# The passage from the bias stage to attention: earlier bias loads, the last third layer moved, another drain order

## What is computed

```
bias = jax.nn.relu(bias @ cpb_w1 + cpb_b1)
bias = jax.nn.relu(bias @ cpb_w2 + cpb_b2)
bias = (bias @ cpb_w3 + cpb_b3).reshape(b, GROUPS, H * W, Hd * Wd)
sim = jnp.einsum('bhid,bhjd->bhij', qh, kh) + bias
attn = jax.nn.softmax(sim, axis=-1)
out = jnp.einsum('bhij,bhjd->bhid', attn, vh)
```

## Time and profile before

| | us |
|---|---|
| time, median of 3 runs (2813.24 to 2814.31) | 2814.09 |
| the profiled execution's own time | 2813.33 |
| its span, first to last instruction | 2811.5 |
| TensorE busy in the span | 2704.1 (96%) |
| VectorE busy | 2146.4 (76%) |
| ScalarE busy | 1669.3 (59%) |
| GpSimd busy | 97.3 (3%) |

### The profile page before, as it was taken

How to read it: one execution, slowest core, us unless ns; L and a number is a source line. 1 busy time by engine, 2 the same in 40 slices (tenths; PEclk the granted TensorE clock), 3 DMA queues, 4 the chain that set the end, 5 groups by cost and what they waited for, 6 DMA issues and landing times. The chain is left out here.

```text
span 2811.5 us, 45931 instructions
## 1 busy us (share of the span) xinstructions
PE 2704.1 (96%) x20105; PEld 1351.6 (48%) x20105; DVE 2146.4 (76%) x1373; ACT 1669.3 (59%) x2594; POOL 97.3 (3%) x132
## 2 busy tenths in 40 slices
PE   5699999999999999999999999999799999999898
PEld 3434434444434444334444344444478888757553
DVE  5799999999999999999999999998552221224364
ACT  4677677776777777777777777776432222201244
POOL 3000000000000000000000000000421000000000
PEclk8899999999999999999999999999999999999999
DMA  1100000000000000001000000100600000200001
GB/s 71 56 16 30 8 29 30 16 29 9 29 29 16 30 9 29 29 16 30 9 29 29 16 29 11 33 7 1 198 1 1 0 1 1 86 0 1 1 1 60
DMA packets 38760, 72.26 MB, mean 26 GB/s; under 512 B 21088, under 2 KB 22048, under 8 KB 36896
## 3 DMA queue, kind: packets, MB, share of 16 engines
q1 hardware_dynamic: 38496, 69.19, 7.5%
q0 software_dynamic: 64, 0.13, 0.0%
HBM read 60.45 MB, written 8.86 MB: 25 GB/s over the span
## 5 line engine op out<-in xcount | busy, mean ns | idle before, releaser
L812 PE MATMUL l_ps<-mlp_w,W2H 128*64 128x512 f16 x5472 | 912.8, 392 | 1.7 <-DVE mlp_w L844 1.7
L889 ACT ACTIVATE relu_top<-l_ps 128x512 f32<-128x512 f32 x1024 | 612.1, 598 | 416.4 <-PE l_ps L812 371.6
L889 ACT ACTIVATE relu_bottom<-l_ps 128x512 f32<-128x512 f32 x1024 | 612.3, 598 | 78.8 <-PE l_ps L812 0.7
L830 DVE SCALAR_TENSOR_TENSOR relu_top<-relu_bottom,sign_ratio,relu_top 128x2048 f32<-128x2048 f32 x256 | 601.4, 2349 | 11.6 <-ACT relu_bottom L889 11.6
L812 PE MATMUL l_ps<-mlp_w,W2L 128*64 128x512 f16 x2736 | 536.0, 388 | 0.0
L812 PEld LDWEIGHTS l_ps<-mlp_w,W2H 128*64 128x64 f16 x5472 | 304.1, 108 | 357.4 <-issue 77.8
L812 PE MATMUL l_ps<-h_words,W2H 128*64 128x512 f16 x2720 | 453.1, 392 | 0.0
L844 DVE TENSOR_TENSOR mlp_w<-words_x,XN 128x2048 f32<-128x2048 f32 x172 | 391.6, 2287 | 24.6 <-PE l_ps L812 24.6
L844 DVE TENSOR_TENSOR mlp_w<-XN 128x2048 f32<-128x2048 f32 x170 | 387.0, 2289 | 19.4 <-PE l_ps L812 19.1
L812 PE MATMUL l_ps<-h_words,W2L 128*64 128x512 f16 x1360 | 266.1, 388 | 0.0
L788 PE MATMUL l_ps<-relu_top,W 128*32 128x512 f32 x2048 | 246.8, 599 | 2.8 <-DVE relu_top L830 2.8
(11 more groups left out here) (389 smaller groups left out, 2696.7 us busy)
## 6 DMA issues: line engine op xcount, KB each, us to landing
XN<-pos_table SPq DMA_DIRECT2D x64, 512.0 KB, 3.7
mlp_w<-in_mlp_w SPq DMA_DIRECT2D x8, 1024.0 KB, 12.6
X<-in_x SPq DMA_DIRECT2D x8, 512.0 KB, 7.6
bias_scratch<-XN SPq DMA_DIRECT2D x64, 64.0 KB, 2.1
mlp_w_hi<-bias_scratch SPq DMA_DIRECT2D x16, 256.0 KB, 3.9
out<-Q SPq DMA_DIRECT2D x16, 256.0 KB, 2.2
XN<-y_pieces SPq DMA_DIRECT2D x96, 12.0 KB
y_rows<-y_pieces SPq DMA_DIRECT2D x96, 12.0 KB
```

The source lines that it names most:

```text
L812: last = nc.tensor.matmul(out[q][a * DH:(a + 1) * DH, :], w[:, half], h[a][:, :, k], start=False, stop=stop, tile_position=(0, a * DH))
L830: nc.vector.scalar_tensor_tensor(tops[i % 3], bots[i % 2][:], K.RHO[:], tops[i % 3], ALU.mult, ALU.add).then_inc(folded, 1)
L889: nc.scalar.activation((bots[i % 2] if d else tops[i % 3])[:, r, BANK * u:BANK * (u + 1)], banks[BANK_OF[c % PER]][:], ACT.Relu).then_inc( ...
```

## The change

- `stage_bias` no longer ends with layers three of doubles 254 and 255, fold 255, the copy and store of pair 15, nor with a wait for all stores. They are functions now (`last_rows_...`), called in `stage_attention`: the fold first on VectorE; the third layers on TensorE behind s 0 and s 1; the copy first on ScalarE; the store first on SP.
- At its end SP of `stage_bias` waits for the stores of 14 pairs (in a total over 15), for the first layers of pairs 0 to 14 and for the coordinate words of all, and loads the bias of four units into four slots, carved from tables that the last pair no longer uses.
- Attention has four bias slots in place of two. The units run in another order (`UNITS`): image 0's four first, then image 1's.
- SP there: store of pair 15 (4 DMAs), output weights, then for units 4 to 7 two bias loads (after the add four units back) and one 1 MB part of MLP weights each; parts 1 and 3; part 0 after six adds, part 2 after eight.
- The drain: TensorE tr g+1 ahead of w g, ScalarE `at` g+1 ahead of merged g; w 5 and w 7 go into score bank 0, whose last scores are added by then. The high part of the first projection tile is made after `at` 6, with merged 3 as its condition. VectorE waits for GpSimd's last multiply before it makes the low part of the output weights.
- Semaphores of an earlier stage are merged (five into two), with the same waits.

The core of the diff. The bodies of `layer_three`, `fold`, `copy_rows` and `store` move out of the engines' functions unchanged, and the removed code of TensorE and ScalarE in attention is in the listing above.

```diff
+UNITS = [c * B + b for b in range(B) for c in range(CC)]
...
+    def last_rows_folded(dve):
+        fold(dve, DBL - 1)
+    def last_rows_summed(pe):
+        layer_three(pe, DBL - 2)
+        layer_three(pe, DBL - 1)
+    def last_rows_copied(act):
+        copy_rows(act, BG - 1)
+    def last_rows_stored(sp):
+        store(sp, BG - 1)
+        return stored, 16 * CH * BG
+    K.last_rows_folded, K.last_rows_summed = last_rows_folded, last_rows_summed
+    K.last_rows_copied, K.last_rows_stored = last_rows_copied, last_rows_stored
+    room = carver(T.x, T.val, T.co[0])
+    K.bias_in = [K.sem(f"bias_in{i}") for i in range(4)]
+    K.bias_slots = [room([P, HALF, PC, J]) for _ in range(4)]
...
-                store(bg)
+                if bg + 1 < BG:
+                    store(sp, bg)
                 if bg + 2 < BG:
                     coords(bg + 2, 0)
                     y_rows(bg + 2)
-            sp.wait_ge(stored, 16 * CH * BG)
+            sp.wait_ge(stored, 16 * CH * (BG - 2))
+            sp.wait_ge(h1, H * (BG - 1))
+            sp.wait_ge(words, JOBS * BG)
+            for g, slot in enumerate(K.bias_slots):
+                for h in range(HALF):
+                    sp.dma_start(slot[:, h], K.db[HALF * UNITS[g] + h].rearrange("(s p) j -> p s j", p=P)).then_inc(K.bias_in[g], 16)
...
@@ the end of the tensor block of stage_bias
-                    layer_three(i - 2)
-                    layer_three(i - 1)
-            layer_three(DBL - 2)
-            layer_three(DBL - 1)
+                    layer_three(pe, i - 2)
+                    layer_three(pe, i - 1)
...
-            for i in range(DBL - 3, DBL):
-                fold(i)
+            for i in range(DBL - 3, DBL - 1):
+                fold(dve, i)
...
-            copy_rows(BG - 1)
@@ stage_attention
-    bi = [room([P, HALF, PC, J]) for _ in range(2)]
+    bi = K.bias_slots
     sc = [room([P, PC, HALF, J]) for _ in range(4)]
+    pr = [room([P, PC, HALF, J]) for _ in range(2)]
     at = [room([P, HW]) for _ in range(2)]
-    pr = [room([P, PC, HALF, J]) for _ in range(2)]
     OW = carver(K.XNB)([P, CC, C])
...
+    LATE = BLK - 3
+    def out_ps(g):
+        return flat(sps[0][:]) if g >= LATE and (g - LATE) % 2 == 0 else ops[:]
...
-            for g in range(BLK):
-                if g >= 2:
-                    sp.wait_ge(added, g - 1)
+            def weights(f):
+                part = slice(f * FC // BLK, (f + 1) * FC // BLK)
+                sp.dma_start(K.WR[:, part], K.dram["mlp_w"][:, part]).then_inc(K.mlp_in, 16)
+            stored, all_stored = K.last_rows_stored(sp)
+            sp.dma_start(OW, K.dram["out_wT"]).then_inc(ow_in, 16)
+            for g in range(len(bi), BLK):
+                sp.wait_ge(added, g - len(bi) + 1)
+                if g == BLK - 1:
+                    sp.wait_ge(stored, all_stored)
                 for h in range(HALF):
-                    sp.dma_start(bi[g % 2][:, h], K.db[HALF * g + h].rearrange("(s p) j -> p s j", p=P)).then_inc(b_in[g % 2], 16)
-                if g == 1:
-                    sp.dma_start(OW, K.dram["out_wT"]).then_inc(ow_in, 16)
-            for g in range(BLK):
-                part = slice(g * FC // BLK, (g + 1) * FC // BLK)
-                sp.dma_start(K.WR[:, part], K.dram["mlp_w"][:, part]).then_inc(K.mlp_in, 16)
+                    sp.dma_start(bi[g % len(bi)][:, h], K.db[HALF * UNITS[g] + h].rearrange("(s p) j -> p s j", p=P)).then_inc(b_in[g % len(bi)], 16)
+                weights(g)
+            for f in (1, 3):
+                weights(f)
+            sp.wait_ge(added, BLK - 2)
+            weights(0)
+            sp.wait_ge(added, BLK)
+            weights(2)
         @block.tensor
         def _(pe):
...
+            def scores(k):
+                if k >= 2:
+                    pe.wait_ge(added, k - 1)
+                for s in range(PC):
+                    last = nc.tensor.matmul(sps[k % 2][:, s], K.Q[:, UNITS[k], s * P:(s + 1) * P], K.KBD[:, UNITS[k]], start=True, stop=True)
+                last.then_inc(s_mm, 1)
+            def weighted(g):
+                pe.wait_ge(t_out, g + 1)
+                if g == LATE:
+                    pe.wait_ge(added, BLK - 1)
+                elif g > LATE:
+                    pe.wait_ge(o_out, g - 1)
+                elif g:
+                    pe.wait_ge(o_out, g)
+                for t in range(NT):
+                    last = nc.tensor.matmul(out_ps(g)[:, t * BANK:(t + 1) * BANK], K.VBD[:, UNITS[g]], at[g % 2][:, t * BANK:(t + 1) * BANK],
+                                            start=True, stop=True)
+                last.then_inc(o_mm, 1)
+            def turned(g):
+                pe.wait_ge(scaled, g + 1)
+                if g >= 1:
+                    pe.wait_ge(t_out, g)
+                for s in range(PC):
+                    last = nc.tensor.transpose(tps[:, s * P:(s + 1) * P], pr[g % 2][:, s].rearrange("p h j -> p (h j)"), K.k("ident"))
+                last.then_inc(t_mm, 1)
+            for k in range(BLK):
+                scores(k)
+                if k == 1:
+                    K.last_rows_summed(pe)
                 if k >= 4:
...
+                    weighted(k - 4)
+                if k >= 3:
+                    turned(k - 3)
+            for g in range(BLK - 4, BLK):
+                if g + 1 < BLK:
+                    turned(g + 1)
+                weighted(g)
...
+            K.last_rows_folded(dve)
...
+            dve.wait_ge(scaled, BLK)
             dve.wait_ge(K.ow_split, 1)
             nc.vector.tensor_tensor(K.ow_lo, OW, K.ow_hi.bitcast(F32), ALU.subtract).then_inc(K.ow_split, 1)
             dve.wait_ge(K.ao_high, 1)
...
+            def merged(g):
+                act.wait_ge(o_mm, g + 1)
+                nc.scalar.activation(K.Q[:, UNITS[g]], out_ps(g), ACT.Copy).then_inc(o_out, 1)
+            def columns(g):
+                act.wait_ge(t_mm, g + 1)
+                if g >= 2:
+                    act.wait_ge(o_mm, g - 1)
+                nc.scalar.activation(at[g % 2], tps[:], ACT.Copy).then_inc(t_out, 1)
+            K.last_rows_copied(act)
+            for k in range(1, BLK + 1):
                 if k >= 5:
...
+                    merged(k - 5)
+                if k >= 4:
+                    columns(k - 4)
+                act.wait_ge(shifted, k)
+                e = flat(sc[(k - 1) % 4][:])
+                nc.scalar.activation(e, e, ACT.Exp).then_inc(ex, 1)
                 if k == 3:
                     act.wait_ge(ow_in, 16)
                     nc.scalar.activation(K.ow_hi, OW, ACT.Copy).then_inc(K.ow_split, 1)
...
+            for g in range(BLK - 4, BLK):
+                if g + 1 < BLK:
+                    columns(g + 1)
+                if g == LATE:
+                    act.wait_ge(o_out, CC)
                     nc.scalar.activation(K.ao_hi(0), K.ao(0), ACT.Copy).then_inc(K.ao_high, 1)
+                merged(g)
```

More of the change, by code:

```diff
@@ L541, in _ @@
             dve.wait_ge(nt_in, 16 * QT)
[L542 to L547, removed]
+            nc.vector.scalar_tensor_tensor(nt2[:], nt[:], OFF_SCALE, K.k("grid_nt"), ALU.mult, ALU.add).then_inc(part, 1)
+            dve.wait_ge(part, ntd + 1)
+            nc.vector.tensor_scalar(nt[:], nt2[:], 2.0, 1.0 / (HD - 1), ALU.mult, ALU.mult).then_inc(part, 1)
+            dve.wait_ge(part, ntd + 2)
+            nc.vector.tensor_scalar(nt2[:], nt[:], -1.0, None, ALU.add).then_inc(part, 1)
+            dve.wait_ge(part, ntd + 3)
             nc.vector.tensor_tensor(pos, K.k("grid_q").unsqueeze(2).to_broadcast([P, ROWQ, J]),
@@ L742, in stage_bias, with layer_three, fold, copy_rows @@
     folded, l3, copied, stored = K.sem("relu2_folded"), K.sem("l3_mm"), K.sem("rows_copied"), K.sem("rows_stored")
+    def layer_three(pe, i):
+        bg, n = divmod(i, PER_BG)
+        pe.wait_ge(folded, i + 1)
+        if bg and n == 0:
+            pe.wait_ge(copied, bg)
+        for q in range(CH):
+            r, u = divmod(q, 2)
+            last = nc.tensor.matmul(p3[32 * q:32 * q + 32, :], K.W3[:, 30 - 2 * n:62 - 2 * n], tops[i % 3][:, r, BANK * u:BANK * (u + 1)],
+                                    start=(n == 0), stop=(n == PER_BG - 1), tile_position=(0, 32 * q))
+        last.then_inc(l3, 1)
+    def fold(dve, i):
+        dve.wait_ge(relu, 2 * CH * (i + 1))
+        nc.vector.scalar_tensor_tensor(tops[i % 3], bots[i % 2][:], K.RHO[:], tops[i % 3], ALU.mult, ALU.add).then_inc(folded, 1)
+    def copy_rows(act, bg):
+        act.wait_ge(l3, PER_BG * (bg + 1))
+        if bg:
+            act.wait_ge(stored, 16 * CH * bg)
+        nc.scalar.activation(br, p3[:], ACT.Identity, bias=K.v("cpb_b3")).then_inc(copied, 1)
+    def store(sp, bg):
+        sp.wait_ge(copied, bg + 1)
+        for q in range(CH):
+            sp.dma_start(K.db[bg].rearrange("(i r u a x) j -> r u i a (x j)", r=2, u=2, a=2, x=W // CH)[q // 2, q % 2],
+                         br[32 * q:32 * q + 32]).then_inc(stored, 16)
+    def last_rows_folded(dve):
```

(5 more changed lines are left out.)

84 lines of the change are left out of this document (12 added, 72 removed).

## The result

| | before | after |
|---|---|---|
| time, median (lowest to highest, 4 runs each), us | 2814.20 (2813.24 to 2815.54) | 2794.49 (2793.38 to 2797.52) |
| ratio, with its 95% interval | | 0.9931 [0.9914, 0.9949] |
| profiled execution: its time, its span, us | 2813.33, 2811.5 | 2794.97, 2793.2 |
| end of the last relu to the projection's first matmul, us | 64.17 | 48.46 |
| from there to the end of the span, us | 769.57 | 766.02 |

What follows compares the result with a forecast made beforehand. TensorE was taken to bound the span, but the changed stretch was read as a chain of waits: 11.8 us from passage and first units plus 4.3 from the drain, 16.1 in all, forecasting 2798.0 us, range 2795.3 to 2803.0.

Steps and rivals of the forecast that it cites:

- Part 1, the start: Passage into attention: first matmul at 1978.1 in place of 1986.35, early bias loads some 90 us earlier costing nothing.
- Part 2, the table load: ScalarE's table load (1.28 us) stands behind the copy, exponential 0 is 0.7 us late; add 2 comes 11.8 us earlier.
- Rival A: Start of attention: the exponential's table load is hidden, 0.7 us less, 2797.3; chance 0.10.
- Part 3, to s 7: Attention from add 2: chain as before, w 0 at 1996.55, s 7 at 2008.0; low clock of 6.9 us costs nothing.
- Part 4, the queue: SP's DMA queue in attention: bias of units 4 to 7 lands in time, margins 1.8, 2.2, 1.7 and 1.2 us.
- Rival B: Attention's DMA queue: interleaved weights make bias 6 and 7 late, 2802.8; chance 0.11.
- Part 5, the drain: End of attention, add 7 to the projection's first matmul: 15.8 us in place of 20.14, 4.3 gained.
- The sum: Last relu to projection: 11.8 us from passage and first units plus 4.3 from the drain, 16.1 in all.
- what lies behind is unchanged and shifts: From the projection's first matmul to the end: no gain or loss, everything only comes earlier.
- a scatter of 0.9 us: Bottom of the range: 0.9 us allowed for scatter, beside 0.7 and 1.1 us of other terms, giving 2795.3.
- Rival C: Start of attention: early loads come late, add 0 3.3 us late, 2801.3 (0.04); or only the drain's 4.3, 2809.8 (0.03).
- rival D: Attention: TensorE stays at 1.2 GHz to the end of the drain, 6.1 us slower, 2820.2; with its like, chance 0.02.

Runs made afterwards that it cites:

- table_first: Changed kernel plus one tiny exponential ahead of the copy of pair 15 on ScalarE, to load the table early: median 2796.69 us, last relu to projection 47.26.
- after_p1: The changed kernel run again unchanged for a third profile: 2797.49 us, last relu to projection 49.72, transposes behind the MLP 8.86.
- high_on_dve: Changed kernel with the high part of the first projection tile made by VectorE, not ScalarE: median 2795.61 us, last relu to projection 49.62.
- low_no_wait: Changed kernel without VectorE's wait for GpSimd's last multiply ahead of the low output weights: last relu to projection 49.55 us.
- weights_last: Changed kernel with MLP weights 4 to 7 issued behind the bias of unit 7, not between units: median 2794.24 us, last relu to projection 49.69.

## Why the prediction was right in its steps and wrong in its number

**Part 1, the start: right.** The early loads were issued 102 us ahead of the last relu's end (90 forecast). The next stage began 0.31 us after the last relu (0.33 taken), add 0 at 2.69 us after it (2.69 forecast, 1980.45 less 1977.76), and the early loads cost nothing that can be seen: the last relu ends at the same time as before, in the mean.

**Part 2, the table load: right.** Exponential 0 at 8.04 (7.8 forecast). The load sits where the gelu's did. By the Trainium skill (ScalarE activation tables: per-element evaluation and per-set limits, section Table sets in the compiler and the runtime: longest runs per block) it would have stood ahead of the copy; the measurement decides against it. Rival A is out, and table_first shows its price: 0.76.

**Part 3, to s 7: right.** w 0 at 18.80 (18.79 forecast), s 7 at 30.26 (30.24). The low clock was half as long as forecast: 1991.3 to 1994.7, 12.6 to 16.0 us after the last relu, where 6.9 us from 11.2 on were allowed. It cost nothing in three of four profiles, as forecast; in the fourth a second piece cost 1.3 us.

**Part 4, the queue: off by 1.6 us.** The bias of unit 7 was forecast 31.0 us after the last relu and was there at 32.6. The output weights landed at 14.4 (13.8 forecast), the bias of units 4, 5 and 6 at 16.8, 21.8 and 26.8 (16.3, 21.2, 26.1): 0.4 to 0.6 late. The last 0.9 us were lost between units 6 and 7. A pair of loads took 5.0 to 5.2 us from issue to issue (1993.03, 1998.01, 2003.19), not 4.9, and SP was held in the issue of a 1 MB part for 3.3 to 3.8 us ahead of unit 7, where before such an issue took 0.4 to 0.9. Of the margin of 1.2 us nothing was left, and add 7 was 0.4 late. Rival B in small.

**Part 5, the drain: right.** 15.78 from add 7 (15.8 forecast), with its parts: multiply 7 at 1.90, `at` 7 behind merged 5, w 7 at 12.42 (12.4).

**The sum.** For the stretch 16.1 was forecast; 15.7 came in the first pair of profiles, 15.9 in the mean of four. The step that failed is the sentence "what lies behind is unchanged and shifts". The term was sized at 0 and measured 3.55 us in the first pair, 2.3 in the mean of four, nearly all of it the clock's fall in the gap behind the MLP (2.87 of 3.55, 2.1 of 2.3). It could have been read from the trace of before, where the gap of 3.1 us and the low clock behind it stand; the prediction looked for low clock only within the changed stretch. The doubt it had there, whether a gap of 3 us brings the clock down, belonged to every such gap behind. With it the range would have reached 3 us lower, to 2792. The bottom of the range was also built on a scatter of 0.9 us, where three runs were known; the fifteen and twenty-one runs of later comparisons spread over 5.5 and 6.0.

That the median fell just outside the range, and not on its edge, is the draw of executions: the eleven of the changed kernel on record have their median at 2795.30, where the range begins. The failed term is not only luck: with the 2.3 us of the mean added to it, that median would be 2797.6 (an estimate), well inside. How much of the 2.3 us was itself drawn stays open.

Rival C is out as a description (the early loads are there), but its price of 3.3 was nearly right when its condition was made: 2.8. Its second price, only the drain's 4.3, did not happen, nor did rival D: in three of the four profiles of the changed kernel the clock was low for 3.4 us of the stretch, in after_p1 for 6.8.

## What to carry over

Where two stages meet at a barrier, list what stands in series there, and move whatever needs only one engine behind the barrier, with the next stage's loads ahead of it; a walk engine by engine from the rows of the trace gave each add and matmul of such a stretch to some 0.5 us. Then look beyond the stretch: where TensorE idled 3.08 us, executions paid 0, 1.3 to 1.7 or 2.9 us, and one kernel did not always pay the same, so a changed kernel's time is not the old one's less the gain, and the range has to hold that. Compare small versions by such a stretch in the profile, not by a median that spreads over 6 us, and look at the clock within it first.

## What the runs showed of the chip that was not expected

- A gap of 3.08 us ahead of 64 transposes cost 0, 1.3 to 1.7 or 2.9 us, and not the same in every execution of one kernel (8.60 and 10.07 us for the transposes before, 7.20 and 8.86 after): the clock did not fall, or was at 1.2 GHz for 3.4 or for 6.8 us.
- With twelve matmuls that nobody needs in that gap the clock stayed up in both profiles.
- VectorE's one-input copy of 1.16 us lengthened a GpSimd multiply from 1.90 to 2.75 us; two inputs and 2.23 us lengthened it to 3.82 (high_on_dve, low_no_wait).
- SP was held 3.3 to 3.8 us in the issue of one 1 MB load when bias loads of short rows (256 B) were ahead of it in the queue. In weights_last it was held 3.3 us in the issue of a bias load at the same place, so it does not take a large load.
